# A selective scan with four product buffers, two more inputs on GpSimd and step sizes added by accumulating transfers

## The chip, the core and the metric

The kernel runs on one NeuronCore of a Trainium2 chip. The metric is the time of one execution on the device in microseconds, as the median of several runs; the engines are TensorE (PE, its weight loads PEld), VectorE (DVE), ScalarE (ACT), GpSimd (POOL) and SyncE (SP), which here only issues transfers.

## What is computed

Sixteen sequences of 1024 tokens with 512 channels pass through a layer norm and a selective scan with 16 states per channel, and then through a block that works on 127 chosen tokens of each group of sequences (attention and MLP), which the change does not touch. The first half, cut to what matters:

```python
xn = layernorm(x)                                   # (16, 1024, 512)
xp = xn @ x_proj_w.T                                # 64 ranks, 16 B, 16 C
delta = softplus(xp[..., :64] @ dt_proj_w.T + dt_b) # (16, 1024, 512)
for t in range(1024):                               # every channel d, state n
    h = exp(delta * A) * h + delta * B * xn
    y = sum_n(h * C)
x1 = x + y + xn * D
```

## The kernel before

**Tiling.** One sequence is a batch. Its 512 channels are 16 chunks of 32; its 16 states are four groups of four. A tile is 32 channels x 4 states = 128 partitions by 1024 steps of time, so a batch has 64 tiles, four a chunk. Channels also come in four blocks of 128 (k = 0 to 3); a block is four chunks.

**A tile's way.** SyncE copies the chunk's 32 rows of `delT` (step size) and `dxT` (step size times input) four times each to `delr` and `dxr` (`repeat`, L242; a chunk's repeat is issued two chunks ahead; it waits for `dx_made[k]` at a block's first chunk). ScalarE makes `decay` = exp(A * delr) in one of two PSUM buffers (`exp_decay`, L587) and copies `dxr` to `dx` in PSUM (`copy_dx`). VectorE multiplies `dx` by `bmat` to `inp` (`make_input`, L706), and scans (`scan`, L718) to `hid`. GpSimd multiplies `hid` by `cmat` to a product `ch` (L873). TensorE sums the states of the product into `ps_y` (`sum_states`, L379), ScalarE copies that to `ysb` (`copy_y`, L604), TensorE transposes it (`turn_y`, L398), and VectorE adds it to the residual rows `xr` (`add_y`, L730, the operation at L737). In chunks named in `OWN_AT` (3 to 13) the input of group 3 is made by GpSimd (`make_input`, L833), at the end of the chunk before.

**The order on each engine** is written out by hand, and waits are on semaphores that count. VectorE: per chunk four scans, the addition of the chunk before between them (after group `YADD`), then the next chunk's inputs; in chunks 2 and 3 also four router sums (L749) each. ScalarE: `copy_y` of the chunk before, decays of groups 2 and 3, `copy_dx` of the next chunk, decays of the next chunk's groups 0 and 1, and at four places of a chunk what `beside` (L639) names: sums for the norms, the copies of the transposed input, and the softplus of a block (`z_half` L489, `exp_log` L507). `z_half` writes |z| to `te` and relu(z) to `dxT`; `exp_log` makes `te` = exp(-|z|), then `tu` and `delT` (log) from it, with a wait before `tu` (L513). For blocks 0 to 2 this is in chunks 12, 13 and 15 of the batch before, for block 3 in chunk 1.

**Step sizes.** The step size of a block is relu(z) + log(1 + exp(-|z|)) with a correction, put together in four steps of GpSimd (`delta`, L841), each over 128x1024: `tu` += `te` (step 0), `delT` += `tu` (1), `delT` += `dxT` (2), `dxT` = `delT` * `xhT` (3). The table `DELTA` (L50) names behind which product (chunk, group) which step of which block stands, with a 1 in front where it is for the next batch. ScalarE may not reuse `te` and `tu` before steps 0 and 1 have read them.

**SyncE's queue** holds, besides the repeats, the stores and loads of whole sequences and, at chunks 14 and 15, the spreading of the next batch's B and C rows over partitions (`spread`, L274: four transfers a group to `bmat` or `cmat`; the first waits for the last input of the group, the second for its last product). It waits in order: what stands behind a waiting repeat is issued later.

**Batches.** The first and the last are written out, the fourteen between them run in a loop of two.

## Time and profile before

| | us |
|---|---|
| median of 3 runs | 4783.68 (4782.91 to 4783.99) |
| the profiled execution | 4781.46 |
| its span, first to last instruction | 4779.6 |
| VectorE busy | 3882.5 (81%) |
| GpSimd busy | 3509.0 (73%) |
| TensorE busy | 2845.7 (60%) |
| ScalarE busy | 2760.5 (58%) |

The shares are of the whole span. The scan phase takes its first three quarters, to about 3700 us; there VectorE and GpSimd fill nearly every slice, and after it TensorE takes over. Busy times count an operation from its start to its end; neighbours on one engine overlap by some 0.05 to 0.1 us, so distances are read from start to start. In the timelines, neighbouring operations of one line are merged (x2, x4), and an engine's idle time ahead of a row stands in brackets with what ended it.

### The profile page before, as it was taken

The numbers are of one execution on the slowest core, as the hardware profiler recorded it, in microseconds if no ns is written. First come the engines' busy times: TensorE is split into PE (matmuls) and PEld (weight loads), VectorE is DVE, ScalarE is ACT, GpSimd is POOL, SyncE is SP. The second block draws the span as 40 slices with busy tenths as digits, with TensorE's granted clock in tenths as the row PEclk, the third lists the DMA queues.
The fourth block names the chain that finished last, engine by engine and source line by source line (L and its number), as shares of the span: only waits on it lengthen the run. The fifth ranks groups of instructions, "written<-read, shape, count | busy, mean of one in ns | idle before, by whom it ended". The sixth has DMA issues, their size and how long they took to land. (4 is left out here: it accounts for less than half of the span.)

```text
span 4779.6 us, 57235 instructions
## 1 busy us (share of the span) xinstructions
PE 2845.7 (60%) x15590; PEld 1061.4 (22%) x15590; DVE 3882.5 (81%) x3322; ACT 2760.5 (58%) x4103; POOL 3509.0 (73%) x1780
## 2 busy tenths in 40 slices
PE   3555454646464555555454645464643299999997
PEld 1111111111111111111111111111110255555553
DVE  3999998999999999999998999899997744444442
ACT  5666766766767676666766666667654222222221
POOL 4999999999999999999999999999996100000000
PEclk7555565656565655556565556565655599999998
DMA  4454545363545455454545463635443300000000
GB/s 102 99 123 119 137 103 153 79 162 86 157 101 142 106 134 129 111 126 115 127 114 142 99 158 73 166 87 155 104 118 84 120 14 18 18 18 18 18 18 7
DMA packets 198209, 472.73 MB, mean 99 GB/s; under 512 B 60688, under 2 KB 61200, under 8 KB 197088
## 3 DMA queue, kind: packets, MB, share of 16 engines
q1 hardware_dynamic: 177136, 452.11, 37.4%
q0 software_dynamic: 20736, 16.88, 1.3%
q8 instruction: 120, 1.97, 0.2%
q14 instruction: 217, 1.78, 0.1%
HBM read 126.83 MB, written 73.43 MB: 42 GB/s over the span
## 5 line engine op out<-in xcount | busy, mean ns | idle before, releaser
L873 POOL TENSOR_TENSOR ch<-hid,cmat 128x1024 f32<-128x1024 f32 x1024 | 2388.1, 2354 | 185.8 <-DMA cmat<-b_and_c 92.2
L727 DVE TENSOR_TENSOR_SCAN hid<-decay,inp 128x1024 f32<-128x1024 f32 x1024 | 2285.5, 2273 | 21.7 <-issue 17.3
L393 PE MATMUL ps_y<-ch,nsum 128*32 128x256 f32 x8192 | 1031.7, 598 | 992.0 <-POOL ch L873 988.3
L594 ACT ACTIVATE decay<-delr,a_neg 128x1024 f32<-128x1024 f32 x1024 | 1131.6, 1113 | 471.7 <-DVE hid L727 469.7
L716 DVE TENSOR_TENSOR inp<-dx,bmat 128x1024 f32<-128x1024 f32 x848 | 981.6, 1212 | 99.1 <-ACT dx L602 63.1
L393 PEld LDWEIGHTS ps_y<-ch,nsum 128*32 128x32 f32 x8192 | 236.8, 142 | 1758.7 <-POOL ch L873 1570.9
L388 PE MATMUL ps_y<-xhT,dskip 128*32 128x256 f32 x2048 | 266.0, 611 | 450.0 <-DVE xr L737 450.0
L609 ACT ACTIVATE ysb<-ps_y 128x256 f32<-128x256 f32 x256 | 97.5, 381 | 570.5 <-PE ps_y L393 559.1
L838 POOL TENSOR_TENSOR inp<-dxr,bmat 128x1024 f32<-128x1024 f32 x176 | 414.8, 2357 | 0.0
L1127 POOL DMA_INDIRECT out_rows<-row,idx_out x16 | 41.3, 2578 | 457.4 <-DVE row L1618 374.1
L376 PE MATMUL aux<-xpT,dtw 64*128 64x512 f32 x256 | 249.4, 1073 | 73.7 <-ACT dxT L504 73.0
L402 PE MATMUL ps_y<-ident,ysb 128*128 128x128 f32 x512 | 159.8, 410 | 181.7 <-ACT ysb L609 163.3
L602 ACT ACTIVATE dx<-dxr 128x1024 f32<-128x1024 f32 x256 | 258.6, 1010 | 3.0 <-DMA dxr<-dxT 3.0
L1189 PE MATMUL ps_t<-w,h2T 128*128 128x512 f32 x512 | 225.8, 599 | 11.9 <-ACT h2T L1328 11.9
L737 DVE TENSOR_TENSOR xr<-xr,ps_y 128x256 f32<-128x256 f32 x256 | 104.1, 406 | 151.4 <-PE ps_y L402 150.1
L1213 PE MATMUL ps_m<-w,gT 128*128 128x512 f32 x512 | 224.9, 592 | 0.0
L1093 POOL COPY idx_x<-cols_i 128x1 uint32 (+1 forms) x16 | 4.6, 286 | 253.3 <-DMA out_rows<-row,idx_out 176.1
L541 ACT ACTIVATE squares<-xr,m 128x512 bf16<-128x512 f32 x256 | 181.6, 712 | 1.1
L847 POOL TENSOR_TENSOR tu<-tu,te 128x1024 f32<-128x1024 f32 x64 | 150.6, 2354 | 36.4 <-ACT tu L518 36.4
L1567 DVE TENSOR_SCALAR GT<-ps_t 128x512 f32<-128x512 f32 x32 | 22.0, 691 | 185.7 <-PE ps_t L1184 185.7
L388 PEld LDWEIGHTS ps_y<-xhT,dskip 128*32 128x32 f32 x2048 | 50.3, 137 | 543.5 <-DVE xr L737 542.0
L367 PE MATMUL aux<-xhT,xproj 128*96 128x512 f32 x256 | 158.2, 742 | 8.2 <-ACT xhT L477 7.5
(167 smaller groups left out, 3863.1 us busy)
## 6 DMA issues: line engine op xcount, KB each, us to landing
dxr<-dxT SPq DMA_DIRECT2D x1024, 128.0 KB, 2.4
delr<-delT SPq DMA_DIRECT2D x1024, 128.0 KB, 2.4
xr<-in_x SPq DMA_DIRECT2D x32, 1024.0 KB, 5.7
bmat<-b_and_c SPq DMA_DIRECT2D x256, 128.0 KB, 3.2
cmat<-b_and_c SPq DMA_DIRECT2D x256, 128.0 KB, 3.7
x_rows<-xr SPq DMA_DIRECT2D x16, 2048.0 KB, 8.1
out_rows<-xr SPq DMA_DIRECT2D x32, 1024.0 KB, 4.4
w<-in_w SPq DMA_DIRECT2D x2, 4096.0 KB, 24.0
```

Source lines behind the costliest of these rows:

```text
L376: pe.matmul(aux[:], dtw[:, k * P:(k + 1) * P], xpT[0:R, h * HALF:(h + 1) * HALF], start=True, stop=True).then_inc(aux_full, 1)
L388: pe.matmul(ps_y[q * CH:(q + 1) * CH, 0:2 * P], dskip[:, k, c % NT * CH:(c % NT + 1) * CH], xhT[:, i, j, q * 2 * P:(q + 1) * 2 * P], start ...
L393: last = pe.matmul(ps_y[q * CH:(q + 1) * CH, 0:2 * P], nsum[:], ch[:, g % 2, q * 2 * P:(q + 1) * 2 * P], start=False, stop=(g == GROUPS - 1))
L541: nc.scalar.activation(squares[:, norm, i % 2], xr[:, par, t, :], ACT.Square, bias=m[:, 1, t:t + 1], accum_out=m[:, 2, t:t + 1])\
L594: nc.scalar.activation(decay[:, g % 2, :], delr[:, c % 2, :], ACT.Exp, scale=a_neg[:, i:i + 1])\
L602: nc.scalar.activation(dx[:], dxr[:, c % 2, :], ACT.Copy).then_inc(dx_ready, 1)
L716: nc.vector.tensor_tensor(inp[:, g, :], dx[:], bmat[:, g, :], ALU.mult).then_inc(inp_ready, 1)
L727: nc.vector.tensor_tensor_scan(hid[:, g, :], decay[:, g % 2, :], inp[:, g, :], 0.0, ALU.mult, ALU.add).then_inc(hid_ready, 1)
L838: nc.gpsimd.tensor_tensor(inp[:, OWN, :], dxr[:, c % 2, :], bmat[:, OWN, :], ALU.mult)\
L873: nc.gpsimd.tensor_tensor(ch[:, g % 2, :], hid[:, g, :], cmat[:, g, :], ALU.mult).then_inc(ch_ready, 1)
L1189: last = pe.matmul(one[bank], xT[:, k, :], w(k), start=(k == 0), stop=(k == n - 1))
L1213: last = pe.matmul(one["m1"], gT[:, k, :], w_2[:, k, :], start=(k == 0), stop=(k == F // P - 1))
```

## The change

Seven things:

- `ch` gets four buffers, one for each group, instead of two. A product waits for the sum of the same group one chunk earlier.
- `OWN_AT` becomes 1 to 13: GpSimd also makes the inputs of group 3 of chunks 1 and 2.
- `YADD` = 2: the addition of a chunk's output stands after the third scan instead of the second.
- `copy_y` stands behind the decays of groups 2 and 3 instead of ahead of them.
- `DELTA` is another table. Blocks 2 and 3 (`BY_DMA`) have their steps 0 to 2 made by transfers that GpSimd's queue issues and that add their source to their destination in SBUF: `delT` += `te`, `delT` += `tu`, `delT` += `dxT`, each waiting for the one before. Three new semaphores count them; ScalarE waits for the first before it writes `te` again (z_half) and for the second before it writes `tu` (exp_log), at blocks 0 and 3.
- SyncE issues `cmat` of groups 0 and 1 for the next batch ahead of chunk 15's repeat, groups 2 and 3 behind it.
- The scratch space for descriptors of GpSimd's transfers is set to 8192 bytes.

```diff
--- before.py
+++ after.py
@@ -27,7 +27,7 @@
 TC = L // P
 KD = D // P
 HALF = 512
-YADD = 1
+YADD = 2
@@ -47,17 +47,18 @@
 Z3 = 1
-DELTA = {(13, 0): (1, 0, 0), (13, 2): (1, 0, 1), (14, 0): (1, 0, 2), (14, 2): (1, 0, 3),
-         (14, 3): (1, 1, 0), (15, 1): (1, 1, 1), (15, 3): (1, 1, 2), (0, 1): (0, 1, 3),
-         (0, 3): (0, 2, 0), (1, 1): (0, 2, 1), (1, 3): (0, 2, 2), (2, 3): (0, 2, 3),
-         (2, 2): (0, 3, 0), (3, 0): (0, 3, 1), (4, 0): (0, 3, 2), (5, 0): (0, 3, 3)}
+DELTA = {(13, 0): (1, 0, 0), (13, 1): (1, 0, 1), (13, 2): (1, 0, 2), (13, 3): (1, 0, 3),
+         (14, 1): (1, 1, 0), (14, 3): (1, 1, 1), (15, 2): (1, 1, 2), (1, 0): (0, 1, 3),
+         (0, 2): (0, 2, 0), (1, 2): (0, 2, 1), (2, 0): (0, 2, 2), (3, 0): (0, 2, 3),
+         (3, 2): (0, 3, 0), (4, 0): (0, 3, 1), (4, 2): (0, 3, 2), (5, 0): (0, 3, 3)}
 RW_COPY = (2, 0)
 ROUTER = (2, 3)
 FINISH1 = (7, 0)
 FINISH2 = (2, 1)
 OWN = GROUPS - 1
-OWN_AT = tuple(range(3, 14))
+OWN_AT = (1, 2, 3, 4, 5, 6, 7, 8, 9, 10, 11, 12, 13)
+BY_DMA = (2, 3)
 ROUTED = (4, 2)
 STORE_LOAD = (3, 4)
@@ -136,7 +137,7 @@
         inp = sb("inp", [P, GROUPS, L])
         hid = sb("hid", [P, GROUPS, L])
-        ch = sb("ch", [P, 2, L])
+        ch = sb("ch", [P, GROUPS, L])
         ysb = sb("ysb", [P, 2 * P])
         delr = sb("delr", [P, 2, L])
         dxr = sb("dxr", [P, 2, L])
@@ -170,6 +171,9 @@
         z_act = sem("z_act")
         delta_step = sem("delta_step")
         stepping = sem("stepping")
+        exp_added = sem("exp_added")
+        rest_added = sem("rest_added")
+        relu_added = sem("relu_added")
         rw_ready = sem("rw_ready")
         ln1 = sem("ln1")
         ln1_act = sem("ln1_act")
@@ -308,6 +312,9 @@
             def body(b, par):
                 final = is_last(b)
                 for c in range(CHUNKS):
+                    if c == CHUNKS - 1 and not final:
+                        for g in range(2):
+                            spread(b + 1, g, 1)
                     if c < CHUNKS - 2:
                         repeat(b, c + 2)
                     elif not final:
@@ -323,9 +330,12 @@
                         load_x(b + 1, 1 - par, STORE_LOAD.index(c))
                     if c == COPY_PROJ[1][0] + 1:
                         store_bc(b + 1)
-                    if c in (14, 15):
+                    if c == CHUNKS - 2:
                         for g in range(GROUPS):
-                            spread(b + 1, g, c - 14)
+                            spread(b + 1, g, 0)
+                    if c == CHUNKS - 1:
+                        for g in range(2, GROUPS):
+                            spread(b + 1, g, 1)
             batches(sp, body)
             store_x1(nb_run - 1, 1)
@@ -391,7 +401,7 @@
                 pe.wait_ge(ch_ready, tile(b, c, g) + 1)
                 for q in range(4):
                     last = pe.matmul(ps_y[q * CH:(q + 1) * CH, 0:2 * P], nsum[:],
-                                     ch[:, g % 2, q * 2 * P:(q + 1) * 2 * P],
+                                     ch[:, g, q * 2 * P:(q + 1) * 2 * P],
                                      start=False, stop=(g == GROUPS - 1))
                 last.then_inc(ch_summed, 1)
@@ -492,7 +502,10 @@
                 if h == 0:
                     if has(b, 1) or k > 0:
-                        act.wait_ge(delta_step, b * KD * 3 + 3 * (k - 1) + 1)
+                        if k == 0 or k == 3:
+                            act.wait_ge(exp_added, b * 32 + (16 if k else 0))
+                        else:
+                            act.wait_ge(delta_step, b * 6 + 3 * (k - 1) + 1)
                         act.wait_ge(z_act, b * KD * ZACT + k * ZACT)
                     if has(b, 1):
@@ -510,7 +523,10 @@
                 act.wait_ge(z_act, n + 2)
                 nc.scalar.activation(te[:], te[:], ACT.Exp, scale=-1.0).then_inc(z_act, 1)
                 if has(b, 1) or k > 0:
-                    act.wait_ge(delta_step, b * KD * 3 + 3 * (k - 1) + 2)
+                    if k == 0 or k == 3:
+                        act.wait_ge(rest_added, b * 32 + (16 if k else 0))
+                    else:
+                        act.wait_ge(delta_step, b * 6 + 3 * (k - 1) + 2)
                 act.wait_ge(z_act, n + 3)
                 nc.scalar.activation(tu[:], te[:], ACT.Identity, bias=1.0).then_inc(z_act, 1)
                 nc.scalar.activation(delT[:, k, :], te[:], ACT.Ln, bias=1.0).then_inc(z_act, 1)
@@ -678,12 +694,12 @@
                 for c in range(CHUNKS):
                     nxt = (b, c + 1) if c < CHUNKS - 1 else (b + 1, 0)
                     beside(b, par, c, 0)
+                    exp_decay(b, c, 2)
+                    exp_decay(b, c, 3)
                     if c > 0:
                         copy_y(b, c - 1)
                     elif has(b, 1):
                         copy_y(b - 1, CHUNKS - 1)
-                    exp_decay(b, c, 2)
-                    exp_decay(b, c, 3)
                     if not (final and c == CHUNKS - 1):
                         copy_dx(*nxt)
                     beside(b, par, c, 1)
@@ -840,7 +856,30 @@
             def delta(b, par, k, step):
-                n = b * KD * 3 + k * 3
+                if k in BY_DMA:
+                    n = (b * len(BY_DMA) + BY_DMA.index(k) + 1) * 16
+                    if step == 0:
+
+                        pool.wait_ge(z_act, b * KD * ZACT + k * ZACT + ZACT)
+                        pool.sem_inc(stepping, 1)
+                        pool.dma_start(delT[:, k, :], te[:], accum_op=ALU.add).then_inc(exp_added, 16)
+                    elif step == 1:
+                        pool.wait_ge(exp_added, n)
+                        pool.sem_inc(stepping, 1)
+                        pool.dma_start(delT[:, k, :], tu[:], accum_op=ALU.add).then_inc(rest_added, 16)
+                    elif step == 2:
+                        pool.wait_ge(aux_emptied, b * NUSE + USE[("z", k, 1)] + 1)
+                        pool.sem_inc(stepping, 1)
+                        pool.wait_ge(rest_added, n)
+                        pool.sem_inc(stepping, 1)
+                        pool.dma_start(delT[:, k, :], dxT[:, k, :], accum_op=ALU.add).then_inc(relu_added, 16)
+                    else:
+                        pool.wait_ge(relu_added, n)
+                        i, j = xhat_slot(k, par)
+                        nc.gpsimd.tensor_tensor(dxT[:, k, :], delT[:, k, :], xhT[:, i, j, :], ALU.mult)\
+                            .then_inc(dx_made[k], 1)
+                    return
+                n = b * 6 + k * 3
                 if step == 0:
                     pool.wait_ge(z_act, b * KD * ZACT + k * ZACT + ZACT)
@@ -868,9 +907,9 @@
                             pool.wait_ge(c_in[g], (b + 1) * 16 * NT)
-                        if has(b, 1) or c * GROUPS + g >= 2:
-                            pool.wait_ge(ch_summed, tile(b, c, g) - 1)
-                        nc.gpsimd.tensor_tensor(ch[:, g % 2, :], hid[:, g, :], cmat[:, g, :],
+                        if has(b, 1) or c > 0:
+                            pool.wait_ge(ch_summed, tile(b, c, g) - GROUPS + 1)
+                        nc.gpsimd.tensor_tensor(ch[:, g, :], hid[:, g, :], cmat[:, g, :],
                                                 ALU.mult).then_inc(ch_ready, 1)
                         if (c, g) in DELTA:
                             ahead, k, step = DELTA[c, g]
@@ -1706,7 +1745,7 @@
     arrays.update(shape_constants(np))
     arrays = {k: np.ascontiguousarray(v) for k, v in arrays.items()}
-    nc = bacc.Bacc("TRN2", target_bir_lowering=False, num_devices=1)
+    nc = bacc.Bacc("TRN2", target_bir_lowering=False, num_devices=1, dynamic_dma_scratch_size=8192)
     a = {k: nc.dram_tensor(f"in_{k}", v.shape, mybir.dt.from_np(v.dtype), kind="ExternalInput").ap()
          for k, v in arrays.items()}
     out = nc.dram_tensor("out_rows", (B, L, D), mybir.dt.float32, kind="ExternalOutput").ap()
```

## Rows read from the trace of the kernel before

**Rows 1.** Busy us by stretch: span, PE, PEld, DVE, ACT, POOL, clock, DMA, GB/s

```profile
80.00:3660.00 3580.00, 1887.33 (x11674) 530.95 (x11674) 3372.59 (x2359) 2424.54 (x3510) 3381.53 (x1640) 0.56 0.48 121
```

**Rows 2.** The page's groups: count | busy us, mean ns | idle before, releaser

```profile
L873 POOL TENSOR_TENSOR ch<-hid,cmat 128x1024 f32<-128x1024 f32 x1024 | 2388.1, 2354 | 185.8 <-DMA cmat<-b_and_c 92.2
```

**Rows 3.** The waits between 1000 and 3000 us: us in total, times, longest

```profile
DVE xr L737 <- PE ps_y L402: 80.0, 53, 3.4
...
POOL ch L873 <- DMA cmat<-b_and_c: 46.1, 8, 7.3
...
POOL ch L873 <- PE ps_y L393: 29.3, 22, 2.6
...
DVE inp L716 <- DMA bmat<-b_and_c: 19.1, 24, 1.1
```

**Rows 4.** VectorE's timeline: start us, us, line, operation, [idle before <-releaser]

```profile
1819.97 4.46 DVE L727 TENSOR_TENSOR_SCAN hid<-decay,inp 128x1024 f32<-128x1024 f32 x2
1824.35 0.40 DVE L737 TENSOR_TENSOR xr<-xr,ps_y 128x256 f32<-128x256 f32 x1
...
1832.42 4.46 DVE L727 TENSOR_TENSOR_SCAN hid<-decay,inp 128x1024 f32<-128x1024 f32 x2
1837.17 0.42 DVE L737 TENSOR_TENSOR xr<-xr,ps_y 128x256 f32<-128x256 f32 x1 [0.29 <-PE ps_y L402]
...
1851.99 0.42 DVE L737 TENSOR_TENSOR xr<-xr,ps_y 128x256 f32<-128x256 f32 x1 [1.13 <-PE ps_y L402]
...
1867.19 0.42 DVE L737 TENSOR_TENSOR xr<-xr,ps_y 128x256 f32<-128x256 f32 x1 [1.42 <-PE ps_y L402]
...
1878.87 4.46 DVE L727 TENSOR_TENSOR_SCAN hid<-decay,inp 128x1024 f32<-128x1024 f32 x2
...
1892.45 4.46 DVE L727 TENSOR_TENSOR_SCAN hid<-decay,inp 128x1024 f32<-128x1024 f32 x2
1899.98 0.42 DVE L737 TENSOR_TENSOR xr<-xr,ps_y 128x256 f32<-128x256 f32 x1 [3.08 <-PE ps_y L402]
...
1909.21 4.46 DVE L727 TENSOR_TENSOR_SCAN hid<-decay,inp 128x1024 f32<-128x1024 f32 x2
1916.31 0.42 DVE L737 TENSOR_TENSOR xr<-xr,ps_y 128x256 f32<-128x256 f32 x1 [2.64 <-PE ps_y L402]
...
1927.54 4.46 DVE L727 TENSOR_TENSOR_SCAN hid<-decay,inp 128x1024 f32<-128x1024 f32 x2
```

**Rows 5.** ScalarE's timeline in chunks 1 and 2 of batch 8

```profile
1899.65 1.01 ACT L602 ACTIVATE dx<-dxr 128x1024 f32<-128x1024 f32 x1
...
1908.87 1.06 ACT L515 ACTIVATE tu<-te 128x1024 f32<-128x1024 f32 x1
...
1915.17 0.36 ACT L609 ACTIVATE ysb<-ps_y 128x256 f32<-128x256 f32 x1
```

**Rows 6.** GpSimd's timeline: first product of chunk 13, last of chunk 14

```profile
1835.64 2.36 POOL L873 TENSOR_TENSOR ch<-hid,cmat 128x1024 f32<-128x1024 f32 x1
...
1861.06 2.34 POOL L873 TENSOR_TENSOR ch<-hid,cmat 128x1024 f32<-128x1024 f32 x1
```

**Rows 7.** SyncE's timeline: the repeat of the next batch's first chunk

```profile
1861.27 2.41 SPq L259 DMA_DIRECT2D dxr<-dxT  x4
```

**Rows 8.** The DMA issues: KB each, median us from issue to landing

```profile
dxr<-dxT SPq DMA_DIRECT2D x1024, 128.0 KB, 2.4
...
xr<-in_x SPq DMA_DIRECT2D x32, 1024.0 KB, 5.7
...
out_rows<-xr SPq DMA_DIRECT2D x32, 1024.0 KB, 4.4
...
out_rows<-row,idx_out POOLq DMA_INDIRECT x16, 15.7
```

**Rows 9.** GpSimd's groups from 3700 to 4780 us: its indirect transfers

```profile
L1127 POOL DMA_INDIRECT out_rows<-row,idx_out x16 | 41.3, 2578 | 457.4 <-DVE row L1618 374.1 <-issue 83.3
L1104 POOL DMA_INDIRECT xg<-x_rows,idx_x x16 | 16.4, 1025 | 13.8 <-POOL idx_x L1093 11.7 <-issue 2.1
```


## The prediction, made before the changed kernel was run

> **What bounds the kernel now.** I read the busy times by stretch first. In the scan phase VectorE and GpSimd are both busy for some 94% of the time, 3373 and 3382 of 3580 us [rows 1], and TensorE and ScalarE are far from it. The phase is 16 batches of 16 chunks, so about 225 us each; what follows it (chosen tokens, from some 3700 us on) isn't touched. With two engines that full, neither's busy time is the answer: the question is which of their waits end last, and at which chunk. So the second view is that of the waits [rows 3]. VectorE stands 80.0 us in 2000 (8.9 batches, so 9.0 us a batch) before the addition L737, for TensorE's transposed output, and 2.1 us a batch for `bmat`; GpSimd stands 5.2 us a batch for `cmat` and 3.3 for TensorE to have summed an older product (two product buffers).
>
> The third view is VectorE's timeline, from chunk 12 of batch 7 to chunk 3 of batch 8 [rows 4]. A chunk in which nothing is late takes 12.45 us with three inputs on VectorE (1819.97 to 1832.42) and 13.58 with four (1878.87 to 1892.45). Two scans take 4.38, so one takes 2.19; the addition takes 0.31, so three inputs take 3.38 and four 4.51. The waits sit in few places: 0.29, 1.13 and 1.42 us in chunks 13 to 15, then 3.08 in chunk 1 and 2.64 in chunk 2. These five are 8.6 of the 9.0 us, and I count 0.5 to 1.6 more for chunks 3 to 11, where no row stands here. The stretch of seven chunks is 107.57 us long.
>
> Behind each lies a different engine. Chunks 14 and 15: GpSimd is late. A product takes it 2.35 us [rows 2], as do its additions; it does both back to back, eleven starts in 25.42 us, so 2.31 a step [rows 6]; the last product of chunk 14 ends at 1863.40 and the addition that hangs on it starts at 1867.19, 3.8 us later (sum, copy, a projection that TensorE has in between, transposes). Chunk 1: the same again, with a step more. Chunk 2: ScalarE is late. From its dx copy at 1899.65 it has no gap up to its output copy at 1915.17 [rows 5], 15.5 us of squares, softplus and decays, and the addition follows 1.14 later.
>
> **The change, part by part.** *Two inputs move* (chunks 1 and 2, group 3) from VectorE to GpSimd: VectorE sheds 2 x 1.13 = 2.3 us a batch, GpSimd takes 2 x 2.31 = 4.6.
>
> *Six additions become transfers.* GpSimd sheds 6 x 2.31 = 13.9 us a batch and issues six accumulating transfers of 512 KB. No row shows one. For the issue, its queue's indirect transfers bound it: 1.02 us for a gather, 2.58 for the scatter [rows 9]; I take 1.0, since a direct transfer computes no addresses from indices and the gathers are the nearer, and below that lies only zero. GpSimd's sum: -13.9 + 4.6 + 6.0 = -3.3 us a batch (+6.2 with the scatter's price).
>
> *How long one takes to land*, T, is the number that matters. Plain transfers on SyncE's queue [rows 8]: 128 KB in 2.4 us, 1 MB in 4.4 (store) and 5.7 (load). Interpolated, plain 512 KB would be 2.4 + 384/896 x 2.0 = 3.3 us. At the far end stands GpSimd's own scatter, 15.7 us. An accumulation must read source and destination, 1 MB, and write 512 KB; that is nearest to the 1 MB load, with 0.3 us for the slower queue: T = 6. The ends are 3.3 and 15.7.
>
> *Four product buffers* take away GpSimd's wait for TensorE: the product that starts at 1835.64 would start at 1834.7, when the one input ahead of it ends and the scan is there. What they cost is memory alone; the space for that queue's descriptors is set to 8192 bytes, and no row prices that: from nothing to a block of GpSimd behind each transfer. I take nothing, since one transfer at a time is in flight.
>
> *Addition after the third scan, output copy after two decays.* In a plain chunk the second scan ends at 4.46, ScalarE's decay follows to 5.5, the copy starts there and the addition 1.14 later, at 6.68. The third scan lets VectorE go at 6.58. So an addition that waited for nothing now waits 0.10 us: plain chunks become 12.55 and 13.7. The wait of up to 2.2 us more that this allows is what covers GpSimd's lag elsewhere.
>
> *Chunks 13 to 15.* The steps for the next batch's blocks 0 and 1 now stand closer: five of them up to the last product of chunk 14 instead of four. GpSimd: 1834.7 + 13 x 2.31 = 1864.7, 1.3 later than before; the addition at 1864.7 + 3.8 = 1868.5; then 0.31 + 2.19 + 4.51, so chunk 0 begins at 1875.5 instead of 1878.87. Within that, the waits for `bmat` must go. SyncE's repeats for the next batch begin at 1861.27 [rows 7], when GpSimd's last step for block 0 is done; it is now done eight steps after the start of chunk 13's first product, 1834.7 + 8 x 2.31 = 1853.2, so `bmat`'s 16 issues behind it come some 5 us earlier relative to their use at the end of chunk 15. `cmat` for groups 0 and 1 is now issued once the products of chunk 15 release it, ahead of the repeat of chunk 1, and has 3 to 4 GpSimd steps (8 us) for a landing of 4: its wait goes too. SyncE's queue then holds the repeat of chunk 1 behind those products; it's wanted a chunk later, so nothing.
>
> *Chunk 0*: 12.55, so chunk 1 begins at 1888.1, 4.4 earlier than before.
>
> *Chunks 1 and 2.* GpSimd's lag no longer reaches the addition. But ScalarE's work is unchanged: its dx copy now starts 5.8 us into chunk 1, 15.5 us later the backlog ends, at 21.3, then the decay for the third scan of chunk 2, which starts at 22.4. From there 1927.54 - 1916.73 + 0.31 = 11.1 to chunk 3: 33.5 us for both, against 35.1.
>
> Here the transfers add a wait. ScalarE's write to `tu` (9.2 us behind the dx copy, at 1908.87; after: 15.0 us into chunk 1) must wait until the transfer that reads `tu` for block 2 has landed. GpSimd issues it after the third product of chunk 1: from 1864.7 six steps to the end of batch 7, three products, an issue of 1.0, six steps: 1864.7 + 15 x 2.31 + 1.0 = 1900.4, 12.3 us into chunk 1. So all of T above 2.7 us stands in ScalarE's full chain, and behind it are queued the log, the squares and the decay on which VectorE's third scan of chunk 2 waits: 6 - 2.7 = 3.3 us a batch. The first transfer, of `te`, is issued at 1885.5 and wanted at 1894.9: hidden up to 9.4 us. The transfers of block 3 (chunks 3 and 4) have a product between them and block only GpSimd, by 1 to 2 us, with some 5 of slack before VectorE notices.
>
> *Sum a batch*: chunk 12 to 3: -5.9 + 3.3 = -2.6; chunks 3 to 11: nine adds of 0.10 against the 1.6 that they lose: -0.7. Together -3.3, times 15 boundaries of batches = -50. The profiled execution has a span of 4779.6 and a time of 4781.5 us, 2.2 below the median of 4783.7: 4781.5 - 50 + 2.2 = **4734**.
>
> **A rule against the row.** The one row of a GpSimd transfer to landing is 15.7 us [rows 8] for a scatter, and it would make this change lose. The Trainium skill, DMA: Bandwidth & Descriptors, section Anatomy of one DMA, fits such transfers as 2.0 us plus bytes at 436 GB/s; for 512 KB that is an estimate of 3.2 us, and the time would be the first rival's. No row here shows a direct transfer of that queue. The Trainium skill, Collectives: The Full Stack, section The bandwidth ceiling, says that a reducing transfer pays for two source reads and not for the addition; by both together the estimate is 4.4 us.
>
> **Rivals.** *The transfer is short* (3.3 us, like a plain one): the stall is 0.6, the sum -6.0 a batch, 4784 - 90 = 4694. For it: plain rates [rows 8]; against it: the double read.
>
> *The transfer is slow*, and the new wait outweighs all. Place: ScalarE's `tu` write in chunk 1 for block 3. It decides from T = 2.7 + 6.6 = 9.3 us, where the sum is zero. At T = 12: +2.7 a batch, 4784 + 41 = 4825. For it: the scatter's 15.7 us, and ScalarE's chain without a gap; against it: the scatter moves rows one by one to HBM.
>
> *It cancels*: the issue costs 2.6 us as the scatter does, which puts the `tu` transfer 1.6 us later, and T is 7.5 to 8, from SyncE's 2 MB store and the repeats on the same engines: -3.3 + 1.6 + 1.7 = 0, 4783.
>
> **How the numbers follow.** Forecast, T from 4 to 8 with issue near 1: 0.53, its own range 4700 to 4765. Short: 0.14, 4694. Cancels: 0.12, 4783. Slow: 0.21, 4800 upwards, 4825 at T = 12. A measurement of this kernel can tell about 0.2%, 9.6 us. Faster 0.66, within 0.2% 0.12, slower 0.22. The range reaches down to the short case and up to the slow one at T = 12: 4682 to 4825.
>
> **What would show it.** Right: the wait of GpSimd for `cmat` and of VectorE for `bmat` nearly gone; plain chunks of 12.55; no wait before the addition in chunk 1; in chunk 2 VectorE idle before its third scan for some 8 to 9 us, released by a decay, with ScalarE idle before its `tu` write (L515 now) for a transfer; GpSimd busy for some 14 us less a batch in additions. Wrong: landing of the accumulating transfers far from 6 us; additions that wait in every chunk for much more than 0.1 us; the third scan of chunk 2 not late; GpSimd's issue much above 1 us.

## The result: no gain, and the profile after

The changed kernel takes 4789.95 us (median of 20 runs, 4784.12 to 4796.85) against 4780.6 of the kernel before (median of 20, 4777.79 to 4783.99): ratio 1.0019, interval 1.0012 to 1.0026. That is 9.4 us slower, at the edge of what a measurement can tell, where 50 us less were forecast. The profiled execution has 4784.12 us, the lowest of the 20, and a span of 4782.3, 2.7 more than that of before.

Both full engines have in fact got less to do. In the same stretch as [rows 1] (columns: stretch, length, busy us of PE, PEld, DVE, ACT, POOL with counts, clock, share of the DMA engines, GB/s):

```profile
80.00:3660.00 3580.00, 1824.87 (x11650) 549.15 (x11654) 3338.56 (x2323) 2414.14 (x3509) 3317.70 (x1671) 0.58 0.56 135
```

VectorE is busy 34 us less, GpSimd 64 us less, and the DMA engines' share has risen from 0.48 to 0.56. The time went into waits. Those between 1000 and 3000 us (us in total, times, longest), to be held against [rows 3]:

```profile
DVE hid L743 <- ACT decay L610: 106.7, 30, 11.1
...
ACT tu L531 <- DMA delT<-tu: 36.8, 9, 5.7
POOL delT L875 <- DMA delT<-tu: 35.5, 12, 4.2
DVE xr L753 <- PE ps_y L412: 26.9, 33, 1.5
ACT squares L551 <- DMA xr<-in_x: 24.7, 9, 3.8
```

VectorE's wait before the addition fell from 80.0 to 26.9 us; the waits for `cmat` (46.1 before) and `bmat` (19.1) are as good as gone, the first 6.2, the second without a row. In their place stands one that before had no row at all: VectorE's scan waits 106.7 us for a decay of ScalarE, in 30 places. Behind it ScalarE waits 36.8 us for the `tu` transfer and 24.7 for the load of the next sequence. Of VectorE's own waits 53 us (addition) and 19 (`bmat`) left, and 107 came.

GpSimd's groups in the same stretch (busy us, mean ns | idle before, what ended it): an issue costs it 0.86 to 1.03 us, as taken, and its step for a third transfer waits for the second one, 3.2 to 4.2 us at block 3 (2.60 in batch 8).

```profile
L912 POOL TENSOR_TENSOR ch<-hid,cmat 128x1024 f32<-128x1024 f32 x566 | 1345.0, 2406 | 91.9 <-DVE hid L743 83.1 <-DMA cmat<-b_and_c 6.2 <-issue 0.4
...
L875 POOL DMA_DIRECT2D delT<-dxT x18 | 18.6, 1031 | 36.3 <-DMA delT<-tu 35.5 <-issue 0.7
L869 POOL DMA_DIRECT2D delT<-tu x17 | 16.7, 980 | 0.0
L865 POOL DMA_DIRECT2D delT<-te x17 | 14.5, 855 | 0.0
```

The mean of a product reads 2406 ns instead of 2354, but from start to start it is still 2.31 us; products near an issue only start earlier inside their neighbour.

VectorE's timeline over the same stretch of batches 7 and 8 as [rows 4], with chunks 6 and 7 behind it (x3: three scans merged):

```profile
1831.14 4.46 DVE L743 TENSOR_TENSOR_SCAN hid<-decay,inp 128x1024 f32<-128x1024 f32 x2
...
1874.40 6.64 DVE L743 TENSOR_TENSOR_SCAN hid<-decay,inp 128x1024 f32<-128x1024 f32 x3
...
1887.02 6.64 DVE L743 TENSOR_TENSOR_SCAN hid<-decay,inp 128x1024 f32<-128x1024 f32 x3
1893.81 0.42 DVE L753 TENSOR_TENSOR xr<-xr,ps_y 128x256 f32<-128x256 f32 x1 [0.15 <-PE ps_y L412]
...
1912.52 2.29 DVE L743 TENSOR_TENSOR_SCAN hid<-decay,inp 128x1024 f32<-128x1024 f32 x1 [8.34 <-ACT decay L610]
...
1923.66 6.64 DVE L743 TENSOR_TENSOR_SCAN hid<-decay,inp 128x1024 f32<-128x1024 f32 x3
...
1951.93 6.64 DVE L743 TENSOR_TENSOR_SCAN hid<-decay,inp 128x1024 f32<-128x1024 f32 x3
...
1964.65 4.56 DVE L743 TENSOR_TENSOR_SCAN hid<-decay,inp 128x1024 f32<-128x1024 f32 x2
1971.49 2.29 DVE L743 TENSOR_TENSOR_SCAN hid<-decay,inp 128x1024 f32<-128x1024 f32 x1 [2.29 <-ACT decay L610]
```

| stretch, us | before [rows 4] | forecast | after |
|---|---|---|---|
| chunk 12 to the start of chunk 1 | 72.48 | 68.1 | 68.5 |
| chunks 1 and 2 | 35.1 | 36.8 | 36.6 |

(Chunk 12 begins one plain chunk ahead of the first row, at 1818.53.) So far this batch goes as forecast within half a microsecond: a plain chunk takes 12.61 us, chunk 1 begins at 1887.02, the addition in it waits 0.15 instead of 3.08, and in chunk 2 the third scan waits 8.34 us for a decay. The loss is seen further on, at 1971.49: 2.29 us in chunk 6, and in the other parity of batches (the loop holds two batches, and odd and even ones differ in what SyncE does when).

The means over batches 1 to 14, worked out from the first scans of all chunks:

| us a batch | before | forecast | after | none by transfer | plain copies |
|---|---|---|---|---|---|
| chunks 12 to 15 and 0 | 74.0 | 69.6 | 69.1 | 69.1 | 69.1 |
| chunks 1, 2 | 34.5 | 36.2 | 37.6 | 34.9 | 35.0 |
| chunks 3, 4 | 27.9 | 28.1 | 28.3 | 28.3 | 28.3 |
| chunks 5, 6 | 26.6 | 25.2 | 27.9 | 27.0 | 26.0 |
| chunks 7 to 11 | 62.3 | 62.8 | 63.0 | 62.9 | 63.0 |

The forecast column is the mean of before with the forecast differences; the last two columns are experiments below. In chunks 1 and 2 the parities differ: even batches went from 35.1 to 36.7, odd ones from 34.0 to 38.5.

### The profile page after: what moved, and what is told of

Read it like the earlier page. It is cut to its first block and busy times, and to the rows that moved or that the text cites. A ratio compares the mean times of both kernels' runs of the same rounds, so it can differ in the third digit from the quotient of the medians.

```text
span 4782.3 us, 57409 instructions
## 1 busy us (share of the span) xinstructions
PE 2783.3 (58%) x15590; PEld 1078.5 (23%) x15590; DVE 3852.8 (81%) x3290; ACT 2751.0 (58%) x4103; POOL 3448.1 (72%) x1812
## 5 line engine op out<-in xcount | busy, mean ns | idle before, releaser
L912 POOL TENSOR_TENSOR ch<-hid,cmat 128x1024 f32<-128x1024 f32 x1024 | 2435.0, 2408 | 173.1 <-DVE hid L743 154.0
L403 PE MATMUL ps_y<-ch,nsum 128*32 128x256 f32 x8192 | 985.8, 587 | 718.0 <-POOL ch L912 715.4
L732 DVE TENSOR_TENSOR inp<-dx,bmat 128x1024 f32<-128x1024 f32 x816 | 941.2, 1211 | 63.0 <-ACT dx L618 63.0
L412 PE MATMUL ps_y<-ident,ysb 128*128 128x128 f32 x512 | 170.2, 434 | 890.2 <-ACT ysb L625 877.1
L403 PEld LDWEIGHTS ps_y<-ch,nsum 128*32 128x32 f32 x8192 | 259.7, 145 | 1422.7 <-POOL ch L912 1150.0
L854 POOL TENSOR_TENSOR inp<-dxr,bmat 128x1024 f32<-128x1024 f32 x208 | 505.5, 2430 | 0.0
L412 PEld LDWEIGHTS ps_y<-ident,ysb 128*128 128x128 f32 x512 | 71.8, 197 | 1116.3 <-ACT ysb L625 1077.1
L386 PE MATMUL aux<-xpT,dtw 64*128 64x512 f32 x256 | 237.0, 1022 | 21.2 <-ACT dxT L517 20.5
L551 ACT ACTIVATE squares<-xr 128x512 bf16<-128x512 f32 x256 | 157.4, 616 | 54.3 <-DMA xr<-in_x 39.1
```

The source lines that it names most:

```text
L386: pe.matmul(aux[:], dtw[:, k * P:(k + 1) * P], xpT[0:R, h * HALF:(h + 1) * HALF], start=True, stop=True).then_inc(aux_full, 1)
L403: last = pe.matmul(ps_y[q * CH:(q + 1) * CH, 0:2 * P], nsum[:], ch[:, g, q * 2 * P:(q + 1) * 2 * P], start=False, stop=(g == GROUPS - 1))
L412: last = pe.transpose(ps_y[:, (2 + t) * P:(3 + t) * P], ysb[:, t * P:(t + 1) * P], ident[:])
L732: nc.vector.tensor_tensor(inp[:, g, :], dx[:], bmat[:, g, :], ALU.mult).then_inc(inp_ready, 1)
L854: nc.gpsimd.tensor_tensor(inp[:, OWN, :], dxr[:, c % 2, :], bmat[:, OWN, :], ALU.mult)\
L912: nc.gpsimd.tensor_tensor(ch[:, g, :], hid[:, g, :], cmat[:, g, :], ALU.mult).then_inc(ch_ready, 1)
```

## Experiments

What the trace of after leaves open is whether the transfers themselves cost the gain (**theory A**: ScalarE's `tu` write waits, and SyncE's queue with its loads is late), or the rest of the change does (**rival B**: the reordering costs, and GpSimd's relief is worth what it brings).

**No transfers.** Same order, buffers and inputs; GpSimd adds for all blocks:

```diff
-BY_DMA = (2, 3)
+BY_DMA = ()
```

> The changed kernel with the step sizes of all four blocks added by GpSimd's own instructions, no accumulating transfers; order, four product buffers and the two moved inputs stay. Theory A (the transfers cost more than they free: ScalarE's tu write in chunk 1 waits 2.2 to 5.7 us for one, and block 3's transfers make SyncE's queue and the second half of the x load late, so ScalarE is late in chunks 5 and 6): chunks 1+2 fall from 37.6 to about 34, chunks 5+6 from 27.9 to about 25.5, the whole to about 4700 us, ratio 0.983. Rival B (GpSimd's work is what counts, and the reordering itself took the gain): GpSimd gets 8 us a batch more, waits before VectorE's additions return, 4790 us or more, ratio 1.002 or above.

4736.46 us, ratio 0.9902 (0.9887 to 0.9917). GpSimd has 8 us a batch more to do (the additions of 13.9 us less the issues of 6), and the kernel is 53 us faster. Rival B is out. Its waits:

```profile
DVE hid L744 <- ACT decay L611: 66.3, 23, 7.3
...
ACT tu L532 <- POOL delT L890: 10.9, 9, 2.6
```

The wait at `tu` is 1.2 us a batch (10.9 in 2000 us). Chunks 1 and 2 take 34.9 as expected within 1 us; chunks 5 and 6 fall only to 27.0, not to 25.5, and that is the larger part of the gap to the 4700 us I expected.

**Transfers for one block only.**

```diff
-BY_DMA = (2, 3)
+BY_DMA = (3,)      # second kernel: (2,)
```

> Transfers for block 3 alone, block 2 added by GpSimd. Theory A: the wait before the tu write goes (to 0.5 us), chunks 1+2 about 34; chunks 5+6 stay near 28. About 4738 us, ratio 0.991. Rival B: between the changed kernel and the one with no transfers, both at or above 1.002.

> Transfers for block 2 alone, block 3 added by GpSimd. Theory A: the tu wait of 2.2 to 5.7 us stays and chunks 1+2 with it near 37.6; SyncE's queue and the x load are on time again and chunks 5+6 fall to about 25.5. About 4752 us, ratio 0.994. Rival B: at or above 1.002. If chunks 5+6 stay at 28, block 3's transfers are not what makes ScalarE late there.

Block 3 alone: 4743.87 us, 0.9921 (0.9908 to 0.9935). Block 2 alone: 4779.08 us, 0.9993 (0.9984 to 1.0002). Chunks 1+2 and 5+6 are 34.6 and 27.9 with block 3 by transfer, 37.9 and 27.0 with block 2. So each block costs where theory A has it, in its own chunks and not in the other's: block 2's transfers 3.0 us a batch in chunks 1 and 2, block 3's 0.9 in chunks 5 and 6. Of the 53 us, block 2's transfers alone make 43 and block 3's alone 7. The waits with block 3 alone:

```profile
POOL delT L876 <- DMA delT<-tu: 30.4, 9, 3.9
ACT squares L552 <- DMA xr<-in_x: 26.7, 9, 4.0
```

ScalarE's wait for the x load (26.7) is there with block 3 alone and has no row with block 2 alone, nor with none.

**Two `tu` buffers.** To make room, groups 1 and 3 share one of three product buffers.

```diff
-        tu = sb("tu", [P, L])
+        tu = sb("tu", [P, 2, L])
...
-                if has(b, 1) or k > 0:
-                    act.wait_ge(rest_added / delta_step of block k - 1)
+                if has(b, 1) or k > 1:
+                    act.wait_ge(the same of block k - 2)
```

> The changed kernel with two tu buffers, so that block 3's write need not wait for block 2's transfer; to make room, groups 1 and 3 share one of three product buffers. All transfers stay. Theory A: no wait before the tu write, chunks 1+2 at 33.6 to 34, the rest unchanged: 4735 us, ratio 0.9905. Rival (that wait only stands in front of another, since the next transfer or GpSimd is late as well): chunks 1+2 stay above 36, 4780 us or more.

4758.57 us, 0.9946 (0.9932 to 0.9959). Chunks 1 and 2 take 33.9, so the `tu` wait was worth 3.8 us a batch. In even batches, from one of which my sum was read, they take 33.8, near its 33.5 without a stall. In odd ones they take 34.0, and took 34.0 in the kernel before. The whole gains only 31 us of the expected 55, since the shared buffer costs 2 us in chunk 14 (GpSimd's wait for TensorE below, which after doesn't have):

```profile
POOL ch L914 <- PE ps_y L405: 45.6, 35, 3.2
```

**Plain copies in the place of accumulations.** The step sizes of blocks 2 and 3 are left out by this.

```diff
-pool.dma_start(delT[:, k, :], tu[:], accum_op=ALU.add)
+pool.dma_start(delT[:, k, :], tu[:])    # and te, dxT alike
```

> The changed kernel with its six transfers a batch copying instead of adding (same sizes, queue, places and waits; the step sizes of blocks 2 and 3 are left out, so the numbers aren't the reference's). What is in dispute is the price of one transfer, 5.2 to 8.1 us to landing with the addition. If the double read makes it (theory A): plain ones land in 3.3 to 4 us, the wait before the tu write falls from 3.7 us a batch to below 1, the whole to about 4745 us. If queue and load beside it make it (rival C): they land in 5 to 8 us as well and the time stays within 10 us of 4790.

4714.33 us, the median of two runs, 0.9862 (0.9844 to 0.988). The rows of its DMA queue and issues (packets, MB, share of the 16 engines; KB each, median us from issue to landing):

```profile
q0 software_dynamic: 34560, 67.22, 4.3%
...
delT<-te POOLq DMA_DIRECT2D x32, 512.0 KB, 4.7
delT<-tu POOLq DMA_DIRECT2D x32, 512.0 KB, 5.0
delT<-dxT POOLq DMA_DIRECT2D x32, 512.0 KB, 4.3
```

The same of the changed kernel:

```profile
q0 software_dynamic: 34560, 67.22, 7.1%
...
xr<-in_x SPq DMA_DIRECT2D x32, 1024.0 KB, 7.3
...
delT<-te POOLq DMA_DIRECT2D x32, 512.0 KB, 6.3
delT<-tu POOLq DMA_DIRECT2D x32, 512.0 KB, 8.1
delT<-dxT POOLq DMA_DIRECT2D x32, 512.0 KB, 5.2
```

And that queue in the kernel with no transfers, where only the gathers and the scatters are left:

```profile
q0 software_dynamic: 20736, 16.88, 1.4%
```

Same bytes, same packets, but twice the time on the engines: (7.1% - 1.4%) of 4782 us are 272 us on each of the 16 for 96 transfers, 2.8 us apiece; copied, (4.3% - 1.4%) of its span, 4711 us, are 137 us, 1.4 apiece. The medians to landing, 5.2 to 8.1 us against 4.3 to 5.0, mix places. At the `tu` transfer of chunk 1, batches 2 to 14, they part:

| us to landing | even batches | odd batches |
|---|---|---|
| accumulating | 5.4 to 6.8 | 7.6 to 8.7 |
| plain copy | 2.9 to 3.0 | 5.2 to 6.6 |

So the 3.3 us for a plain one and the 6 for an accumulating one both held where little else was under way, and neither theory had it wholly: there the addition costs some 3 us, in the odd batches 2, and what runs beside it 2 to 3 more. With plain copies chunks 5 and 6 fall to 26.0 in the mean, 25.2 in the odd batches, which is what I had forecast for them. The copy also relieves GpSimd, whose issue of one takes 0.58 us instead of 0.98 (its group between 1000 and 3000 us):

```profile
L869 POOL DMA_DIRECT2D delT<-tu x18 | 10.5, 583 | 0.0
```

So this run doesn't take apart what the shorter transfer and what the shorter issue bring to those chunks.

**The reordering undone** in the kernel with no transfers:

```diff
-YADD = 2
+YADD = 1
...
+                    copy_y of the chunk before
                     exp_decay(b, c, 2)
                     exp_decay(b, c, 3)
-                    copy_y of the chunk before
```

> The kernel with no transfers, with the output copy again ahead of the decays and the addition after the second scan. Theory D (ScalarE's backlog sets chunks 1+2 either way, so the reordering gains only GpSimd's slack at chunks 14 and 15 and loses 0.16 us in each plain chunk): chunks 1+2 stay at 34.5 to 35.5, plain chunks return to 12.45, chunks 13 to 15 grow by 1 to 2 us; 4736 us within 15. Rival E (the reordering is worth what it was to remove, 3.1 us in chunk 1 and 1.4 in chunk 15): 30 to 60 us slower than 4736.

4781.31 us, 1.0003 (0.9994 to 1.0012): 45 us slower than with it. Rival E has the time and theory D fails: without the reordering nothing is left of the gain. Theory D was nearly right on chunks 1 and 2, though (34.3), and rival E wrong on the places. The 0.16 us a plain chunk that it costs are there (12.45 again), but the wait before the addition is back, 15.3 us a batch instead of 4.1:

```profile
DVE xr L754 <- PE ps_y L413: 136.1, 57, 5.0
```

Most of it stands in chunks 5 (15.7 instead of 13.1) and 14 (16.8 instead of 13.9), where GpSimd is late, not in chunk 1.

**Two product buffers** in the kernel with no transfers:

```diff
-ch = sb("ch", [P, GROUPS, L])        # and ch[:, g] where it is used
+ch = sb("ch", [P, 2, L])             # ch[:, g % 2]
-pool.wait_ge(ch_summed, tile(b, c, g) - GROUPS + 1)
+pool.wait_ge(ch_summed, tile(b, c, g) - 1)
```

> The kernel with no transfers and two product buffers instead of four, order as changed. The third product of a chunk must then wait until the first is summed, which TensorE can't begin before the addition at 6.7 us: about 1.3 us of waiting for GpSimd a chunk. Theory: the reordering needs the four buffers, GpSimd's period rises by some 10 to 20 us a batch, the whole to 4850 or more. Rival: GpSimd has that slack, 4736 within 15.

4791.4 us, 1.0023 (1.0014 to 1.0033), 55 us slower than with four. The direction holds, the size doesn't: GpSimd waits 3.6 us a batch, not 10 to 20, and the batch is 3.4 us longer, in chunks 14, 1 and 2. That it is late elsewhere anyway and so finds its buffer free would explain the small size; no run shows it.

```profile
POOL ch L913 <- PE ps_y L404: 31.8, 34, 2.1
```

**ScalarE's backlog taken out of chunk 1.** With no transfers chunk 2 still takes 22.2 us, where scans, inputs and router sums need 15.7. Seven square sums and the inverse deviation go to chunk 2, the output rows to chunks 3 and 4, block 2's first two steps some products earlier:

```diff
-SUMS2 = {..., (1, 0): range(8, 10), (1, 1): range(10, 12), (1, 2): range(12, 14), (1, 3): range(14, 17)}
+SUMS2 = {..., (1, 0): range(8, 10), (2, 1): range(10, 12), (2, 2): range(12, 14), (2, 3): range(14, 17)}
-FINISH2 = (2, 1)
+FINISH2 = (3, 0)
-MAKE_OUT = ((3, 1), (3, 1), (3, 2), (3, 2), (3, 3), (3, 3), (3, 3), (3, 3))
+MAKE_OUT = ((3, 2), (3, 2), (3, 3), (3, 3), (4, 1), (4, 1), (4, 2), (4, 2))
```

> The kernel with no transfers, with ScalarE's work taken out of chunk 1: the last seven square sums and the inverse deviation of the second norm move to chunk 2, the output rows to chunks 3 and 4, and block 2's steps 0 and 1 of GpSimd two and three products earlier. Theory A/D: what is left in chunk 2 is ScalarE's backlog alone, chunks 1+2 fall from 34.9 to 29 or so, and GpSimd, 218 us a batch, becomes the bound: 4685 us, ratio 0.979. Rival (something else holds the third scan of chunk 2, or GpSimd's lag from chunk 0 takes the gain): chunks 1+2 above 33, 4725 us or more.

4707.66 us, 0.985 (0.9836 to 0.9863). Chunks 1 and 2 fall to 29.8 as expected: it was ScalarE's backlog. Chunk 5 grows from 13.1 to 16.3, GpSimd being late; what the stall in chunk 2 had hidden comes out there.

**GpSimd relieved, ScalarE's sums spread further.** First the inputs of chunks 4 and 5 go back to VectorE and block 3's steps 1 to 3 stand later; then the first norm's sums also begin in chunk 4, and those of the sequence's first half no longer wait for the load of the second:

```diff
-OWN_AT = (1, 2, 3, 4, 5, 6, 7, 8, 9, 10, 11, 12, 13)
+OWN_AT = (1, 2, 3, 6, 7, 8, 9, 10, 11, 12, 13)
...
-SUMS1 = {(5, 1): range(0, 2), (5, 2): range(2, 4), (5, 3): range(4, 8), (6, 0): range(8, 10), (6, 1): range(10, 12), (6, 2): range(12, 14), (6, 3): range(14, 17)}
+SUMS1 = {(4, 3): range(0, 2), (5, 1): range(2, 4), (5, 2): range(4, 6), (5, 3): range(6, 8), (6, 1): range(8, 10), (6, 2): range(10, 13), (6, 3): range(13, 17)}
```

> The kernel with ScalarE's work spread (no transfers), with GpSimd's inputs of chunks 4 and 5 given back to VectorE (11 a batch, as in the kernel before, but chunks 1 to 3 and 6 to 13) and block 3's steps 1 to 3 each some products later. Theory F (with ScalarE's backlog gone GpSimd's work, 218 us a batch, is the bound, and its lag shows as the 3.4 us of chunk 5): chunk 5 falls from 16 to about 13.6, GpSimd sheds 4.6 us a batch and VectorE takes 2.3: about 4665 us, ratio 0.976. Rival: the lag only moves to chunks 13 to 15, 4700 us.

> The same, with the first norm's sums over the first half of a sequence begun in chunk 4 and spread to chunk 6, so that no sums stand ahead of chunk 6's decays. Theory A (ScalarE's sums make chunk 6 late, 13.9 instead of 12.6): another 1.3 us a batch, about 4647 us. Rival (the second half of the x load is then what ScalarE waits for): no gain.

4688.17 us, 0.9807 (0.979 to 0.9823), and 4662.02 us, 0.9751 (0.9735 to 0.9767). Chunk 5 falls to 12.6 in the first, chunk 6 from 14.2 to 12.6 in the second. The first gains 19 us where 43 were expected: chunk 5 gives 3.6 us a batch, but the inputs in chunks 3 and 4 take 2.3 and chunk 6 another 0.4, where ScalarE now waits for the load. The second changed the sums' places and their wait at once, so which of the two did it isn't shown. The wait for a decay, in the second:

```profile
DVE hid L745 <- ACT decay L612: 19.5, 23, 1.8
```

With the input of chunk 4 on GpSimd again:

```diff
-OWN_AT = (1, 2, 3, 6, 7, 8, 9, 10, 11, 12, 13)
+OWN_AT = (1, 2, 3, 4, 6, 7, 8, 9, 10, 11, 12, 13)
```

> The best kernel so far (sums spread, no transfers) with the input of chunk 4 on GpSimd again, 12 a batch. Theory F (GpSimd's lag decides from chunk 4 on): VectorE sheds 1.1 us in chunk 3, GpSimd takes 2.3; if GpSimd still has that slack the whole falls by 17 us to 4645; if not, chunk 5 grows by about as much, 4662 within 5.

4659.15 us, 0.9742 (0.9725 to 0.9758), the fastest here and 131 us below the changed kernel, though not clearly below the one with 11 inputs: chunk 3 falls by 1.1 us, chunk 5 grows by 0.4, chunks 7 and 8 by 0.2 and 0.4. The other branch of the expectation, 4662 within 5, is what came.

**The transfers where ScalarE has slack.** The kernel of 4662 us with the six accumulating transfers and 13 inputs on GpSimd:

```diff
-OWN_AT = (1, 2, 3, 6, 7, 8, 9, 10, 11, 12, 13)
-BY_DMA = ()
+OWN_AT = (1, 2, 3, 4, 5, 6, 7, 8, 9, 10, 11, 12, 13)
+BY_DMA = (2, 3)
```

> As the kernel before this in the list, but with the six accumulating transfers and GpSimd's 13 inputs. GpSimd has 4 us a batch less than without transfers. Theory A (a transfer costs where ScalarE or SyncE's loads stand behind it, and here the tu write comes at 12.7 us into chunk 1, the tu transfer some 5 us earlier): ScalarE waits 1 to 3 us for tu, the loads are late again in chunks 5 and 6: 4670 to 4700 us, slower than without. Rival G (once ScalarE has slack the transfers pay, since they relieve GpSimd): 4640 us or less.

4677.7 us, 0.978 (0.9764 to 0.9796), 16 us slower than without. Theory A holds for this pair, which differs in two things, the transfers and two inputs on GpSimd; transfers with 11 or 12 inputs were not tried. The same two waits stand there, and the one for a decay is up from 19.5 to 44.6:

```profile
ACT squares L552 <- DMA xr<-in_x: 42.9, 11, 5.2
...
DVE hid L745 <- ACT decay L612: 44.6, 29, 4.9
...
ACT tu L532 <- DMA delT<-tu: 21.4, 9, 4.0
```

## Why the prediction was wrong

**What held.** ScalarE reaches the `tu` write 15.0 us into chunk 1 in batch 8, as forecast; GpSimd issues the `tu` transfer at 11.8 (12.3 forecast) and pays 1.0 us for it. ScalarE's timeline in batch 8:

```profile
1904.93 1.06 ACT L531 ACTIVATE tu<-te 128x1024 f32<-128x1024 f32 x1 [2.91 <-DMA delT<-tu]
...
1962.12 0.63 ACT L551 ACTIVATE squares<-xr 128x512 bf16<-128x512 f32 x1 [3.36 <-DMA xr<-in_x]
```

GpSimd's, in the same batch:

```profile
1898.81 1.01 POOL L869 DMA_DIRECT2D delT<-tu  x1
```

1904.93 - 1898.81 = 6.1 us for the landing, the T = 6 of the sum, and 2.91 us of waiting in front of it. `cmat` and `bmat` cost next to nothing any more; plain chunks are 12.61 (12.55 forecast). That a scan in chunk 2 would wait 8 to 9 us for a decay was named as the sign.

The chunks from 12 to 0 gained 4.9 us a batch against 4.4 forecast, and that is partly luck: the boundary that was read, from an odd to an even batch, gained 4.0, and those from an even to an odd one, which the sum hadn't looked at, 5.7.

**Where the miss sits.** The forecast was -3.3 us a batch, the batches measured +0.5. Of these some 4 us, 2.7 are in chunks 5 and 6 and 1.4 in chunks 1 and 2; the additions, at 0.16 instead of 0.10 us each, make 0.3 in chunks 3, 4 and 7 to 11, and chunks 12 to 0 give 0.5 back.

**What failed in chunks 1 and 2: T was taken as one number, and one batch for all.** T is 6 us in the even batches and some 8 in the odd ones. GpSimd's timeline in batch 9:

```profile
2124.53 1.12 POOL L869 DMA_DIRECT2D delT<-tu  x1
```

ScalarE's, in the same batch:

```profile
2132.19 1.06 ACT L531 ACTIVATE tu<-te 128x1024 f32<-128x1024 f32 x1 [4.73 <-DMA delT<-tu]
```

7.7 us to landing, 4.73 of waiting. SyncE's, ahead of both:

```profile
2117.04 0.42 SPq L239 DMA_DIRECT2D x_rows<-xr  x1
```

In the odd batches from 3 to 13 the 2 MB store of x1 is issued some 5 us into chunk 1, in the even ones within 0.6 us of its start (1887.48 below). So in the odd ones the store, or the repeats queued behind it, still run when the `tu` transfer starts. Two batches that break the alternation bear this out. In batch 1 the store goes out 0.2 us into the chunk, and T is 6.0. In batch 8 of the kernel with block 2's transfers alone the store takes 14.0 us, past the issue of the transfer, and T is 8.7 in an even batch. With plain copies the alternation is left (in batches 3 to 14, 0.0 to 0.3 us of waiting in the even ones, 1.9 to 3.6 in the odd), although the store lands there just before the `tu` transfer starts; the repeats behind it land after. Store and repeats were not taken apart by a run of their own.

So the stall became 3.8 us a batch instead of 3.3. The larger part of these chunks' 1.4 us, 0.9, is that without a stall they gain only 0.7 instead of 1.6: in odd batches ScalarE's backlog sets them as before (34.0 and 34.0), and the 35.1 of the sum was read in an even one.

**What failed in chunks 5 and 6, and is larger: "the 1.6 that they lose", and that block 3's transfers "block only GpSimd, by 1 to 2 us, with some 5 of slack before VectorE notices".** The forecast had chunks 3 to 11 gain 0.7 us a batch; they lost 2.4, most of it in chunks 5 and 6 (+1.3 against -1.4). That their waits would go was assumed without a row. In the kernel before, the wait of 1.2 us is in chunk 6, before the addition, and GpSimd is behind it: ScalarE itself sat idle until TensorE had the last product's sum, and TensorE had waited 1.22 us for that product. ScalarE's and VectorE's timelines before, in batch 8:

```profile
1972.73 0.38 ACT L609 ACTIVATE ysb<-ps_y 128x256 f32<-128x256 f32 x1 [2.38 <-PE ps_y L393]
```

```profile
1973.89 0.42 DVE L737 TENSOR_TENSOR xr<-xr,ps_y 128x256 f32<-128x256 f32 x1 [1.21 <-PE ps_y L402]
```

The same chunk of the kernel without transfers, reordered:

```profile
1953.66 0.38 ACT L626 ACTIVATE ysb<-ps_y 128x256 f32<-128x256 f32 x1 [1.18 <-PE ps_y L404]
```

```profile
1954.83 0.42 DVE L754 TENSOR_TENSOR xr<-xr,ps_y 128x256 f32<-128x256 f32 x1 [1.31 <-PE ps_y L413]
```

So the reordering leaves this wait as it is, and chunks 5 and 6 take 27.0 there. GpSimd has no slack in them. To remove the wait it would have to be relieved, and the transfers of block 3 give it little: GpSimd stands 3.4 us a batch for the second of them to land (30.4 us in 9 places with block 3 alone) and is still late in chunk 5, where the addition waits 0.9 us in the mean.

And in chunk 6 the transfers put another wait in the place of GpSimd's. The prediction priced them on the engines that wait for them, ScalarE and GpSimd, and nowhere on the 16 DMA engines, where each takes 2.8 us, nor on SyncE's queue, whose issues take longer while other transfers are under way. SyncE's timeline after, in batch 8:

```profile
1887.48 1.70 SPq L239 DMA_DIRECT2D x_rows<-xr  x1
1889.79 6.86 SPq L263 DMA_DIRECT2D dxr<-dxT  x4
...
1944.96 4.07 SPq L267 DMA_DIRECT2D delr<-delT  x4
1949.30 0.40 SPq L243 DMA_DIRECT2D out_rows<-xr  x1
1955.06 0.39 SPq L232 DMA_DIRECT2D xr<-in_x  x1
```

The same of the kernel before, in its chunks 4 and 5:

```profile
1948.67 2.42 SPq L263 DMA_DIRECT2D delr<-delT  x4
1951.34 0.39 SPq L239 DMA_DIRECT2D out_rows<-xr  x1
1955.90 0.40 SPq L228 DMA_DIRECT2D xr<-in_x  x1
```

In chunk 4 four issues took 4.07 us instead of 2.42. The load of the next sequence's second half waits until the store of the output rows that it overwrites has landed, 5.8 us after its issue instead of 4.6. So it goes out 15.7 us after the start of chunk 4 (1939.32), before it was 12.9, and lands in 6.5 us instead of 5.0. ScalarE has its sums of that half in chunk 5, stands 3.36 us for it (row 1962.12 above), is late in chunk 6, and VectorE's third scan there waits 2.29 us (means: 2.4 in the even batches, 1.4 in the odd). With one block at a time, only block 3 brings this wait.

Only with plain copies are the two chunks down to 25.2, and that in half of the batches. In batch 9 there ScalarE makes its sums at the same places, and the scan waits 0.17 us. So the sums alone, which my expectation for the kernel with the sums spread had held for the cause of chunk 6's wait, don't make it; they do when the load is late.

**The rivals.** The slow transfer had the right mechanism and, as the kernels with one block each show, 3.0 us a batch of it are real, but T in chunk 1 came nowhere near 9.3 (8.7 at most). The rival that cancels had nearly the right sum by partly wrong terms: it took an issue of 2.6 us, which measured 1.0, and named the store and the repeats as what lengthens T, which fits. A T of 7.7 in half of the batches measured as 0.5 us a batch in the mean, not the 1.7 of its sum, and chunks 5 and 6 stand in none of the rivals. The rule of the Trainium skill (DMA: Bandwidth & Descriptors, Anatomy of one DMA) gives an estimate of 3.2 us for 512 KB; a plain copy from this queue took 2.9 to 3.0 in the even batches and 5.2 to 6.6 beside other traffic in the odd. The other one (Collectives: The Full Stack, The bandwidth ceiling), that a reducing transfer pays for a second source read, agrees with the engine time: 2.8 against 1.4 us. The 4.4 us by both together were too low: it took 5.4 to 6.8 in the even batches.

Not settled is why the unprofiled runs of the changed kernel spread over 13 us, where those of the kernel without transfers lie within 1.1, and why its median is 6 us above the profiled one. The kernel with block 2's transfers alone spreads alike (4774.6 to 4786.3), so a landing time that varies from run to run in front of ScalarE's full chain would do it; no run takes this apart.

## What to carry to other kernels

Work that moves from a full engine to the DMA queues has two prices, and the engine's own issue is the small one: ask which engine waits for the landing and whether that one has a gap there, and what else is under way on the same 16 engines, above all loads that some other engine wants right after. An accumulating transfer counts twice in that (2.8 against 1.4 us on each engine). Read a wait in both parities of a loop before you count it for all batches, and ask of each wait that is to go which engine is late behind it. And before two full engines are relieved further, look for the stretch in which a third one, 58% busy over all, has no gap: here spreading ScalarE's sums over neighbouring chunks brought 29 us alone and over 70 with GpSimd's load fitted to it, without the transfers.

## What the runs showed of the hardware

- An accumulating SBUF-to-SBUF transfer of 512 KB takes 2.8 us on each of the 16 DMA engines, a copy of the same size 1.4.
- To landing it took 5.4 to 6.8 us where the 2 MB store was out early, the copy 2.9 to 3.0; where the store and the repeats behind it came late, 7.6 to 8.7 and 5.2 to 6.6.
- The issue cost GpSimd 0.86 to 1.03 us in the mean of a group, near a gather's 1.02 [rows 9]; that of the copy 0.58.
- SyncE's issue of a 128 KB transfer, 0.6 us otherwise, takes 1.4 us and more behind a 2 MB store: four of them took up to 5.4 us in the kernel without transfers and 6.86 with an accumulating one under way as well.
